# The attention vector rides in front of the turned x, and two warming products are left out

## What is computed

```python
# layer 0, attention over edges of kind 1
e      = einsum("bid,bjd->bij", x * a_0[:, 0], x)        # scores of all pairs
scores = where(adj == 1, leaky_relu(e, 0.2), -9e15)
x      = layernorm(x + softmax(scores) @ x)
# layer 1, one relation
h      = x @ W_loop.T
g      = h @ Wg_loop.T
vals   = (h + b_loop) * sigmoid(g + bg_loop)
x      = layernorm(x + relu(adj.T @ vals))
```

## Time and profile before

| | before |
|---|---|
| median of 3 runs | 108.2 us (108.18 to 108.44) |
| the profiled execution, its own time | 107.89 us |
| its span, first to last instruction | 106.1 us |
| outside the span | 1.8 us |
| busy: PE, DVE, ACT, POOL | 96.3, 94.7, 86.9, 74.0 us |
| mean granted TensorE clock | 0.989 of 2.4 GHz |

### The profile page before, as it was taken

The page is one execution under the profiler, slowest core; times in us unless marked ns, Lnnn a source line. Parts: engine busy times, 40 slices in busy tenths (PEclk is TensorE's granted clock), DMA queues, the critical chain, the costliest instruction groups (busy, mean ns, idle before and its releaser), DMA issues.

```text
span 106.1 us, 2745 instructions
## 1 busy us (share of the span) xinstructions
PE 96.3 (91%) x682; PEld 88.1 (83%) x682; DVE 94.7 (89%) x380; ACT 86.9 (82%) x217; POOL 74.0 (70%) x130
## 2 busy tenths in 40 slices
PE   6997996999999999999999999999999999799600
PEld 6965796899999999999999999999989999678300
DVE  0189999999999899999999999999998999898990
ACT  5257889899999999999798989999699879798200
POOL 5025657367355999899999995989998881857560
PEclk9999999999999999999999999999999999999995
DMA  2999999999997319805630306030303030331625
GB/s 57 311 397 364 388 346 302 367 331 349 347 343 201 120 52 284 256 4 135 165 104 0 99 3 180 24 99 0 90 9 99 9 105 0 99 93 44 166 59 142
DMA packets 22530, 17.36 MB, mean 164 GB/s; under 512 B 1265, under 2 KB 18418, under 8 KB 22514
## 3 DMA queue, kind: packets, MB, share of 16 engines
q1 hardware_dynamic: 22370, 17.18, 53.1%
q10 hardware_dynamic: 144, 0.00, 0.1%
HBM read 12.98 MB, written 4.19 MB: 162 GB/s over the span
## 4 chain that ended last, share of the span: by engine, by line
PE 72%; DVE 13%; DMA 4%; issue 4%; POOL 2%; ACT 1%; SPq 1%; DVEq 0%; POOLq 0%; ACTq 0%
PE p_hg L1201 23%; PE p_o L1172 13%; PE p_ag L1221 11%; PE p_e L1142 10%; PE p_ut L1161 6%; PE p_yt L1188 6%; DMA inputs<-x_t 4%; DVE nscore L1007 3%; PE p_e L1145 2%; DVE out_s L1080 2%; POOL rs L817 2%; DVE rel L989 1%; DVE res L1063 1%; DVE st L1099 1%; DVE res L1022 1%
## 5 line engine op out<-in xcount | busy, mean ns | idle before, releaser
L1201 PE MATMUL p_hg<-w_both,y_t 128*128 128x256 f32 x128 | 30.5, 380 | 0.0
L1201 PEld LDWEIGHTS p_hg<-w_both,y_t 128*128 128x128 f32 x128 | 23.1, 190 | 2.5
L898 ACT ACTIVATE prob<-nscore,nmax 128x128 f32<-128x128 f32 x64 | 20.2, 394 | 0.6 <-DVE nmax L1007 0.4
L817 POOL TENSOR_TENSOR rs<-rs,minus_half 128x8 f32<-128x8 f32 x12 | 20.2, 1686 | 0.0
L1022 DVE SCALAR_TENSOR_TENSOR res<-p_o,rz,inputs 128x128 f32<-128x128 f32 x64 | 18.0, 344 | 1.0 <-ACT y L915 0.3
L1172 PE MATMUL p_o<-inputs,prob_t 128*128 128x129 f32 x128 | 17.0, 275 | 0.1
L1221 PE MATMUL p_ag<-vals,mask 128*128 128x128 f32 x116 | 15.5, 276 | 1.0 <-ACT mask L874 0.7
L1172 PEld LDWEIGHTS p_o<-inputs,prob_t 128*128 128x128 f32 x128 | 15.9, 191 | 0.5 <-issue 0.3
L1221 PEld LDWEIGHTS p_ag<-vals,mask 128*128 128x128 f32 x116 | 14.5, 191 | 1.7 <-ACT mask L874 0.9
L1142 PE MATMUL p_e<-inputs,xat 128*128 128x128 f32 x104 | 13.9, 276 | 0.8 <-DVE nmax L1007 0.8
L1142 PEld LDWEIGHTS p_e<-inputs,xat 128*128 128x128 f32 x104 | 12.9, 192 | 1.2 <-DVE nmax L1007 1.0
(11 more groups left out here) (97 smaller groups left out, 170.8 us busy)
## 6 DMA issues: line engine op xcount, KB each, us to landing
inputs<-x_t SPq DMA_DIRECT2D x16, 256.0 KB, 5.3
inputs<-adj_rows SPq DMA_DIRECT2D x16, 256.0 KB, 5.5
inputs<-x SPq DMA_DIRECT2D x16, 256.0 KB, 6.5
out<-out_s SPq DMA_DIRECT2D x14, 256.0 KB, 2.4
out<-out_s SPq DMA_DIRECT2D x4, 128.0 KB, 1.9
w_rows<-w SPq DMA_DIRECT2D x1, 128.0 KB, 2.9
wg_s<-wg_t SPq DMA_DIRECT2D x1, 128.0 KB, 4.1
w_rows<-w SPq DMA_DIRECT2D x1, 64.0 KB, 4.4
```

The source lines that it names most:

```text
L817: nc.gpsimd.tensor_tensor(rs[:, k, 1], rs[:, k, 0], minus_half[:], ALU.pow).then_inc(rstd1_done, 1)
L898: nc.scalar.activation(prob[:, k, i], nscore[:, k, i], ACT.Exp, scale=-1.0, bias=nmax[:, k, i:i + 1]).then_inc(exp_done, 1)
L1201: last = nc.tensor.matmul(p_hg[:, 2 * h + i], y_t[:, g % 2, part(g, h)][:, i], w_both[:], start=True, stop=True)
```

## The change

The array of turned x gets 16 columns in front. It becomes one two-dimensional array `a_x_t` of 128 rows by 16 + 64 * 128 floats: 15 zeros, then the float of `a_0`, then turned x of all graphs. The tile `inputs` gets 16 columns (64 bytes) at the same place, and `a_col` is now the last of them. The first transfer of SP carries 528 floats (2,112 bytes) to each partition where it carried 512 (2,048). The transfer on ACT, its tile and its semaphore go away, and whoever weighs x waits for the first group's transfer in their place. In the memory of the chip the row of a partition is now 32,832 bytes long, where it was 32,768. The warming products are 7, where they were 9.

```diff
@@
+FRONT = 16
@@ def program
-def program(nc, x, x_t, adj, adj_rows, a_0, a_all, w, wg_t, b_loop, b_fwd, b_bwd, out):
+def program(nc, x, a_x_t, adj, adj_rows, a_all, w, wg_t, b_loop, b_fwd, b_bwd, out):
+    x_t = a_x_t[:, FRONT:].rearrange("p (g d) -> p g d", d=P)
@@
-        a_col = sb("a_col", [P, 1])
@@
-        inputs = sb("inputs", [P, n_graphs * (3 * P + 1)])
-        xt_at = n_graphs * (P + 1)
+        inputs = sb("inputs", [P, n_graphs * (3 * P + 1) + FRONT])
+        front_at = n_graphs * (P + 1)
+        xt_at = front_at + FRONT
         adj_at = xt_at + n_graphs * P
-        x_all = inputs[:, 0:xt_at].rearrange("p (g d) -> p g d", d=P + 1)
+        x_all = inputs[:, 0:front_at].rearrange("p (g d) -> p g d", d=P + 1)
+        front = inputs[:, front_at:xt_at]
+        a_col = front[:, FRONT - 1:FRONT]
@@
-        a_loaded = sem("a_loaded")
@@ SP, load_scores
-                sp.dma_start(xt_all[:, graphs(g)], x_t[:, graphs(g)]).then_inc(xt_loaded[g], 16)
+                if g == 0:
+                    sp.dma_start(inputs[:, front_at:xt_at + SIZES[0] * P], a_x_t[:, 0:FRONT + SIZES[0] * P])\
+                        .then_inc(xt_loaded[0], 16)
+                else:
+                    sp.dma_start(xt_all[:, graphs(g)], x_t[:, graphs(g)]).then_inc(xt_loaded[g], 16)
@@ weigh of POOL, ACT and DVE alike
-                dve.wait_ge(a_loaded, 16)
+                dve.wait_ge(xt_loaded[0], 16)
                 dve.wait_ge(xt_loaded[g], 16)
@@ ACT
-            nc.scalar.dma_start(a_col[:], a_0).then_inc(a_loaded, 16)
@@ PE
             pe.wait_ge(warm_ready, 1)
-            for i in range(9):
+            for i in range(7):
                 nc.tensor.matmul(p_ag[:, 0], warm[:], warm[:], start=True, stop=True).then_inc(warmed, 1)
@@ the arrays that are handed over
+    def a_and_x_t(a, of):
+        x_t = np.transpose(np.asarray(of), (2, 0, 1)).reshape(P, -1)
+        return np.concatenate([np.zeros((P, FRONT - 1), x_t.dtype), np.asarray(a), x_t], axis=1)
```

More of the change, by code:

```diff
@@ L738, in weigh @@
             def weigh(g):
-                pool.wait_ge(a_loaded, 16)
+                pool.wait_ge(xt_loaded[0], 16)
                 pool.wait_ge(xt_loaded[g], 16)
@@ L745, in weigh @@
                                         xt_all[:, graphs(g)].rearrange("p g d -> p (g d)"),
-                                        a_col[:].broadcast_to([P, n * P]), ALU.mult).then_inc(xat_by_p, 1)
+                                        a_col.broadcast_to([P, n * P]), ALU.mult).then_inc(xat_by_p, 1)
             def norm1(g):
@@ L877, in weigh @@
             def weigh(g):
-                act.wait_ge(a_loaded, 16)
+                act.wait_ge(xt_loaded[0], 16)
                 act.wait_ge(xt_loaded[g], 16)
@@ L881, in weigh @@
                     act.wait_ge(e_done, g - XATS + 1)
-                nc.scalar.activation(xat[:, g % XATS, 0:SIZES[g]], xt_all[:, graphs(g)], ACT.Copy, scale=a_col[:])\
+                nc.scalar.activation(xat[:, g % XATS, 0:SIZES[g]], xt_all[:, graphs(g)], ACT.Copy, scale=a_col)\
                     .then_inc(xat_by_s, 1)
@@ L981, in weigh @@
                 nc.vector.tensor_scalar(xat[:, g % XATS, 0:SIZES[g]].rearrange("p g d -> p (g d)"),
-                                        xt_all[:, graphs(g)].rearrange("p g d -> p (g d)"), a_col[:], None, ALU.mult)\
+                                        xt_all[:, graphs(g)].rearrange("p g d -> p (g d)"), a_col, None, ALU.mult)\
                     .then_inc(xat_by_v, 1)
@@ L1252 @@
     arrays = {
-        "x": x, "x_t": np.transpose(np.asarray(x), (2, 0, 1)), "adj": adj,
-        "adj_rows": rows(adj), "a_0": L0_gnn_a_0,
+        "x": x, "a_x_t": a_and_x_t(L0_gnn_a_0, x), "adj": adj,
+        "adj_rows": rows(adj),
         "a_all": np.concatenate([L0_gnn_a_0, L0_gnn_a_1, L0_gnn_a_2, L0_gnn_a_3], axis=1),
```

## The result

The changed kernel is slower: 110.15 us, the median of 6 runs (109.05 to 112.53), beside 108.32 us for the kernel before; ratio 1.0124, 95% interval 1.0072 to 1.0177. In some runs of most kernels TensorE's clock falls a second time, near 13 us; the ratios leave out the runs far above the fastest of their kernel, while medians and ranges are over all runs. The first profile of the changed kernel (112.53 us, span 110.7) is of an execution with such a fall, so e5's profile of the same kernel (span 107.4) stands beside it. One of the first six, 110.59 us, has the mean clock of such a fall too (0.963) and still counts in 1.0124; the other three that count give about 1.010.

The account below looks back on a forecast made before the run. PE's fixed block of work bounds the kernel, fed by the second transfer of turned x. Saving 0.45 less 0.02 for the longer first transfer gives 0.43 us: 108.2 to 107.8 us, range 107.4 to 108.7 us.

Parts of the forecast that it names:

- The change gains something only if the transfers of turned x and adjacency themselves land earlier: At the kernel's beginning: an earlier vector alone gains nothing, since DVE then waits longer for the second transfer of turned x.
- moves by the same 0.43 us: ACT's wait for the adjacency of groups 2 and 3, until 9.23 us before, was to end 0.43 us earlier.
- The vector's own transfer, 0.45 us: Between 2.3 and 3.6 us: removing the vector's small packets, which hold engines at 219 GB/s, saves 0.45 us.
- what is saved ahead of that is saved for every later transfer of the queue: From 3.7 us on the DMA engines are full, so the saving was to reach all later transfers: 0.43 us.
- The new rows are harder to read: Rival: rows off even places slow each turned x transfer by 0.08 us; 108.0 us, no change; chance 0.16 with cut packets.
- Two zeros fewer: Start of PE: seven warming products instead of nine free PE as the weighed tile comes, gap some 0.1 us; no gain alone.
- The late clock: Rival: PE's pause before group 0 keeps it at 1.2 GHz longer; relu at 6.5 us, total 108.7 us; chance 0.13.
- Kept, the products of group 0 would cap the gain: With nine warming products, group 0's products would be ready at 6.2 us, capping the gain near zero.
- The chances: Whole kernel: faster 0.50, same 0.33, slower 0.17.

Follow-up runs that it names:

- e5: The changed kernel measured again, unaltered, beside the kernel before: 108.89 us, ratio 1.0048.
- e2: The changed kernel with 9 warming products instead of 7, the array part alone: 108.93 us, ratio 1.0050 to the kernel before.
- e8: The changed kernel with 64 columns in front instead of 16, rows on 256 bytes, big tile in its old place, 7 warming products: 108.40 us, ratio 1.0006.
- straight rows: The changed kernel with every group's turned x starting on 256 bytes in memory, only the first transfer 64 bytes ahead; two measurements: 108.35 us (0.9954), 108.53 us (1.0003).
- e4: The kernel before without the vector's transfer, a_col filled with ones by DVE, 9 warming products: ratio 1.0033.
- e6: The kernel before with turned x shifted by 16 floats in memory only, rows 32,832 bytes apart: 109.02 us, ratio 1.0081.
- e15: The changed kernel with every group's turned x starting on 256 bytes in memory, 7 warming products, first measurement: 108.35 us, ratio 0.9954.
- e1: The kernel before with 7 warming products instead of 9, nothing else changed: median 109.26 us, ratio 0.998.
- e17: The changed kernel with straight rows and 9 warming products instead of 7: 108.68 us, ratio 0.9986 to the kernel before.
- e3: The changed kernel with 64 columns in front instead of 16, rows on 256 bytes, big tile in its old place, 9 warming products: 108.50 us, ratio 1.0015.
- e12: The changed kernel with 64 columns in front, 7 warming products, rows of turned x and adjacency 1,024 floats longer in memory: 108.53 us, ratio 0.9981.

## Why the prediction was wrong, point by point

- *"The change gains something only if the transfers of turned x and adjacency themselves land earlier"*: right. The loss came by that road, 0.5% by the ratios of e2 and e5. But the landing that decided was another than the one I priced: I followed the second transfer of turned x, and in e2 and e8 the chain starts with the adjacency of group 3, which in my words "moves by the same 0.43 us". With straight rows it came at 9.65 and 9.79 us, no earlier than before's 9.23.
- *The vector's own transfer, 0.45 us*: in the changed kernel not even the first gain came (first weighing at 4.32 us, 183 GB/s), as its rows were off. With rows in place it was right in size at the first transfer (0.42 us in e4, from 4.23 to 3.81 us; 3.58 to 3.84 us in nine profiles with no vector transfer and the rows of turned x in place, 4.12 to 4.42 us in the seven that keep it). The step that failed is **"what is saved ahead of that is saved for every later transfer of the queue"**. 0.09 us was left one weighing later. I took the share of 1.00 from 3.7 us on for a fixed rate of work; with an early start the same stretch ran at 266 GB/s in place of 355.
- *"The new rows are harder to read"*: this rival named the cause and was mis-sized. It took 0.08 us more for each transfer of turned x, at most 0.32 us up to the adjacency of group 3, so the sum put the rows at nothing. Over the runs they cost 0.5% (e2, 0.5 us) to 0.8% (e6, 0.6 to 0.9 us); e6's profile has 0.90 us at that adjacency (10.13 against 9.23 us), part of it the spread. Since I let it only eat a gain, it was booked as no change.
- *Two zeros fewer*: the pause was forecast at 0.1 us for a tile at 3.61 us. With the shifted rows the tile came at 4.32 us, and PE paused for 0.81 us in the profile shown. The late clock then did what that rival described (relu of group 0 at 7.46 us, I had 6.5). I gave it 0.13, and made it independent of the rows; but the shifted rows bring the tile later (4.32 us, 3.62 in e15), and so lengthen the pause. The pause alone does not settle it: e5's profile has one of 0.78 us and an early clock. Its price was too low by itself, 108.7 us where the three runs of e1 took 109.64 to 110.07, and the second fall of the clock was not in it: the profiled run with both took 112.53.
- *"Kept, the products of group 0 would cap the gain"*: e17 keeps nine zeros with straight rows and reads no different from seven (0.9986 beside 0.9954 and 1.0003 of the kernel before), so with straight rows the zeros capped nothing.
- The chances: 0.50 on faster hung on two steps that no row of before showed.

## What to carry to other kernels

When something small is put in front of a large array, look at where every later row then starts in memory and how far apart the rows are: 64 bytes in front shifted 4 MB of rows and cost 0.5%, and 48 more unused floats gave that back. A transfer gained at the start is worth only what is left at the transfer on which the chain hangs, so price a gain at that transfer. Before reading a landing time as an effect, see how far it moves between executions of the same program; here that was 0.8 us, more than the whole forecast. Warming work is set against the moment at which the first real tile arrives; move one and the other has to be set again, over many runs, since what it seems to change is how often the clock is late.

## What the hardware showed that was not expected

- The alternating packets of four bytes kept the engines at 219 GB/s (0.75 busy); without them they ran at 340 (0.98), and then at 266 where before had 355. What takes the lead back is open: neither rows off a power of two apart (e3, e12) nor the missing vector (e4) changed it.
- Turned x starting 64 bytes in, with rows 32,832 bytes apart: a dip to 298 GB/s (e6) between 6 and 8 us with engines idle. Why there, and why in engines that wait, was not settled, nor which of the two, start or distance, does it.
- The clock's rise did not come at one moment in kernels with equal work ahead of it: loads turn from 333 to 192 ns at 4.6 us in before, between passes of group 0 in e2, and only after group 0 in e4. Fewer zeros seem only to shift the odds.
- A second fall of the clock costs some 2.6 us in a quarter of the runs of the kernel before. It follows a gap on PE near 12 us wherever it was profiled, and with four products of zeros there none of 11 runs had it.
